# Band selections of a tile in two goes over eight heads each, instead of four goes over four

## What is computed

```python
scores = jnp.einsum('bqhd,bkhd->bhqk', q, k) / jnp.sqrt(d)   # 8 heads, 256 queries, 256 keys
band = jnp.abs(idx[:, None] - idx[None, :]) <= local_size    # 64
scores = jnp.where(band[None, None], scores, neg)
attn = jax.nn.softmax(scores, axis=-1)
o = jnp.einsum('bhqk,bkhd->bqhd', attn, v).reshape(n, t, e)
```

## Time and profile before

| | us |
|---|---|
| median of 3 runs | 968.19 |
| lowest and highest | 966.16, 969.89 |
| span of the profiled execution, first to last instruction | 963.8 |

### The profile page before, as it was taken

How to read it: one execution, slowest core, us unless ns; L and a number is a source line. 1 busy time by engine, 2 the same in 40 slices (tenths; PEclk the granted TensorE clock), 3 DMA queues, 4 the chain that set the end, 5 groups by cost and what they waited for, 6 DMA issues and landing times.

```text
span 963.8 us, 25212 instructions
## 1 busy us (share of the span) xinstructions
PE 871.5 (90%) x9945; PEld 506.2 (53%) x9945; DVE 852.0 (88%) x1719; ACT 740.0 (77%) x1299; POOL 817.8 (85%) x1133
## 2 busy tenths in 40 slices
PE   6588989999999999999999999999999998888874
PEld 3244455555555555555555555555555555544432
DVE  3998888899999999999999999999999998888553
ACT  2546477788888888888888888888888887777751
POOL 4777689999999999999999999999999997656741
PEclk9889899999999999999999999999999999999997
DMA  8000000112211222212112222222212112112233
GB/s 269 1 18 13 7 24 24 29 31 46 47 41 40 51 52 52 51 41 51 39 38 50 51 48 44 51 51 52 51 41 52 39 32 44 41 40 49 46 67 76
DMA packets 109668, 45.59 MB, mean 47 GB/s; under 512 B 89840, under 2 KB 108528, under 8 KB 109552
## 3 DMA queue, kind: packets, MB, share of 16 engines
q1 hardware_dynamic: 109552, 44.00, 20.0%
HBM read 14.09 MB, written 4.19 MB: 19 GB/s over the span
## 4 chain that ended last, share of the span: by engine, by line
DVE 44%; PE 40%; issue 6%; ACT 3%; DMA 2%; SPq 2%; POOL 2%; POOLq 0%; DVEq 0%; ACTq 0%
DVE rowmax L2596 8%; PE ps L592 6%; PE ps L757 6%; PE ps L481 5%; DVE hsplit L2669 4%; DVE prob_a L2534 4%; DVE hid L2656 4%; DVE amax L2525 4%; PE ps L556 3%; PE ps L667 3%; PE ps L723 3%; PE ps L538 3%; PE ps L619 2%; DVE rot L2505 2%; PE ps L677 2%
## 5 line engine op out<-in xcount | busy, mean ns | idle before, releaser
L2596 DVE TENSOR_REDUCE rowmax<-ps 128x4 f32<-128x768 f32 x256 | 243.2, 950 | 23.3 <-PE ps L619 22.6
L1515 ACT ACTIVATE prob<-ps 128x768 f32<-128x768 f32 x256 | 206.9, 808 | 44.5 <-PE ps L647 44.1
L2076 POOL TENSOR_TENSOR hsum<-hsum,minus_half 128x32 f32<-128x32 f32 x32 | 175.7, 5491 | 7.9 <-DVE hsum L2516 7.9
L2113 POOL TENSOR_SCALAR_AFFINE_SELECT prob<-prob 128x256 f32<-128x256 f32 (+1 forms) x256 | 138.5, 541 | 32.2 <-ACT prob L1515 32.2
L2115 POOL TENSOR_SCALAR_AFFINE_SELECT prob<-prob 128x512 f32<-128x512 f32 (+1 forms) x256 | 147.5, 576 | 0.0
L667 PE MATMUL ps<-prob,v_pad 128*32 128x192 f32 x2048 | 103.8, 331 | 1.6 <-POOL prob L2115 1.6
L1490 ACT ACTIVATE high<-ps,bx_col 128x512 f16<-128x512 f32 x128 | 95.2, 769 | 9.1 <-PE ps L592 3.8
L619 PE MATMUL ps<-k_rows,q_rows 24*128 24x192 f16 x1024 | 87.4, 249 | 8.6 <-DVE rowmax L2596 6.7
L647 PE MATMUL ps<-q_rows,k_rows 25*128 25x192 f16 x1024 | 86.8, 247 | 3.2 <-ACT prob L1515 2.5
L592 PE MATMUL ps<-x,wx_qk 64*128 64x256 f32 x512 | 73.4, 404 | 11.5 <-DVE prob_a L2534 11.4
L742 PE MATMUL ps<-wgu,xsplitT 128*128 128x512 bf16 x256 | 66.4, 382 | 12.2 <-ACT v_pad L1501 9.2
(11 more groups left out here) (153 smaller groups left out, 2233.2 us busy)
## 6 DMA issues: line engine op xcount, KB each, us to landing
v_swap<-v_own SPq DMA_DIRECT2D x64, 68.0 KB, 2.0
xin<-in_x SPq DMA_DIRECT2D x32, 128.0 KB, 2.1
enc<-in_ctx SPq DMA_DIRECT2D x32, 128.0 KB, 2.2
out<-yout SPq DMA_DIRECT2D x32, 128.0 KB, 2.0
prob<-in_w_guT SPq DMA_DIRECT2D x4, 512.0 KB, 7.6
prob<-in_w_projT SPq DMA_DIRECT2D x2, 512.0 KB, 9.8
hT<-hsplit SPq DMA_TRANSPOSE x64, 3.1
q_rows<-in_Wkv SPq DMA_DIRECT2D x1, 512.0 KB, 4.0
```

The source lines that it names most:

```text
L1515: copy(prob[:, 2 * c:2 * c + 2, :, :].rearrange("p u a b -> p u (a b)"), ps[:, STB:STB + 2, 0:2 * QW], ACT.Exp, scale=float(XD) ** -0.5).t ...
L2076: g.tensor_tensor(hsum[:, 1, :], hsum[:, 0, :], minus_half[:, :], ALU.pow).then_inc(S["head_pow3"], 1)
L2113: g.affine_select(out=lead, in_=lead, compare_op=ALU.is_ge, fill=0.0, base=BAND - 64 * kb, pattern=[[0, 4], [1, cut]], channel_multiplier=-1)
L2596: v.tensor_reduce(of_head[:, hq:hq + 2, 2 * ng:2 * ng + 2], ps[:, MXB:MXB + 2, 0:2 * QW].rearrange("p j (a b) -> p j a b", a=2), AX, ALU.m ...
```

## The change

`do_sel` covers eight units per call, and a tile has two calls. Each call still issues four affine_selects, now with 512, 1024, 1024 and 512 elements per partition. The first call waits for exp call 4 and the second for exp call 8. In POOL's lists the old calls 0 and 2 are taken out, and the new calls stand where the old calls 1 and 3 stood. `do_val` waits by itself for selection c // 2 + 1 of its tile, so calls 0 and 1 wait for the first and calls 2 and 3 for the second. The order of PE's, DVE's, ACT's and SP's lists is the same.

```diff
             def do_val(t, c):
...
+                pe.wait_ge(S["sel"], t.at(2, c // 2 + 1))
                 g = c % 2
...
             def put_val(t, c):
-                pe.wait_ge(S["sel"], t.at(4, c + 1))
                 do_val(t, c)
...
             def do_sel(t, c):
-                u = slice(4 * c, 4 * c + 4)
+                u = slice(8 * c, 8 * c + 8)
                 for kb, cut in ((0, 64), (1, 128)):
                     lead, trail = prob[:, u, kb, 0:cut], prob[:, u, kb, cut:QW]
                     g.affine_select(out=lead, in_=lead, compare_op=ALU.is_ge, fill=0.0,
-                                    base=BAND - 64 * kb, pattern=[[0, 4], [1, cut]], channel_multiplier=-1)
+                                    base=BAND - 64 * kb, pattern=[[0, 8], [1, cut]], channel_multiplier=-1)
...
             def put_sel(t, c):
-                pool.wait_ge(S["exp"], t.at(8, 2 * c + 2))
+                pool.wait_ge(S["exp"], t.at(8, 4 * c + 4))
                 do_sel(t, c)
...
-                t = at(-7)
-                if t:
-                    put_sel(t, 0)
                 t = at(-5)
                 if t:
                     put_y1_pow(t)
...
                 t = at(-7)
                 if t:
-                    put_sel(t, 1)
+                    put_sel(t, 0)
...
-                t = at(-7)
-                if t:
-                    put_sel(t, 2)
...
                 t = at(-7)
                 if t:
-                    put_sel(t, 3)
+                    put_sel(t, 1)
```

POOL's prologue for tiles 0 to 2, from the change. The lines with a minus are the old calls:

```diff
-            pool.wait_ge(S["exp"], tile[0].at(8, 2))
+            pool.wait_ge(S["exp"], tile[0].at(8, 4))
             do_sel(tile[0], 0)
-            pool.wait_ge(S["exp"], tile[0].at(8, 4))
-            do_sel(tile[0], 1)
...
-            do_sel(tile[0], 2)
             do_y1_pow(tile[3])
             pool.wait_ge(S["exp"], tile[0].at(8, 8))
-            do_sel(tile[0], 3)
+            do_sel(tile[0], 1)
...
-            pool.wait_ge(S["exp"], tile[1].at(8, 6))
-            do_sel(tile[1], 2)
             pool.wait_ge(S["variance"], tile[6].at(1, 1))
             do_head_pow3(tile[6])
             pool.wait_ge(S["y2_stats"], tile[0].at(1, 1))
...
             do_qkn(tile[6])
             pool.wait_ge(S["exp"], tile[1].at(8, 8))
-            do_sel(tile[1], 3)
-            pool.wait_ge(S["exp"], tile[2].at(8, 2))
-            do_sel(tile[2], 0)
+            do_sel(tile[1], 1)
             pool.wait_ge(S["qk"], tile[7].at(1, 1))
             pool.wait_ge(S["qkn"], tile[6].at(1, 1))
             do_rotated(tile[7])
             pool.wait_ge(S["exp"], tile[2].at(8, 4))
-            do_sel(tile[2], 1)
+            do_sel(tile[2], 0)
```

More of the change, by code:

```diff
@@ L1087, in _ @@
             do_o_ps(tile[3])
-            pe.wait_ge(S["sel"], tile[0].at(4, 1))
             do_val(tile[0], 0)
@@ L1109, in _ @@
             do_proj_ps(tile[2], 2)
-            pe.wait_ge(S["sel"], tile[0].at(4, 2))
             do_val(tile[0], 1)
@@ L1129, in _ @@
             do_tr_ps(tile[0], 0)
-            pe.wait_ge(S["sel"], tile[0].at(4, 3))
             do_val(tile[0], 2)
@@ L1157, in _ @@
             do_mx(tile[2], 4)
-            pe.wait_ge(S["sel"], tile[0].at(4, 4))
             do_val(tile[0], 3)
@@ L1167, in _ @@
             do_tr_ps(tile[0], 1)
-            pe.wait_ge(S["sel"], tile[1].at(4, 1))
             do_val(tile[1], 0)
@@ L1191, in _ @@
             do_maxT_ps(tile[2])
-            pe.wait_ge(S["sel"], tile[1].at(4, 2))
             do_val(tile[1], 1)
@@ L1200, in _ @@
             pe.wait_ge(S["ot0"], tile[1].at(1, 1))
-            pe.wait_ge(S["sel"], tile[1].at(4, 3))
             do_val(tile[1], 2)
@@ L1221, in _ @@
             do_pt_ps(tile[5], 0)
-            pe.wait_ge(S["sel"], tile[1].at(4, 4))
             do_val(tile[1], 3)
@@ L1244, in _ @@
             do_aT_ps(tile[5])
-            pe.wait_ge(S["sel"], tile[2].at(4, 1))
             do_val(tile[2], 0)
@@ L1261, in _ @@
             do_mx(tile[3], 6)
-            pe.wait_ge(S["sel"], tile[2].at(4, 2))
             do_val(tile[2], 1)
@@ L1284, in _ @@
             do_val(tile[2], 2)
-            pe.wait_ge(S["sel"], tile[2].at(4, 4))
             do_val(tile[2], 3)
@@ L1328, in _ @@
             do_st(tile[31], 4)
-            pe.wait_ge(S["sel"], tile[31].at(4, 1))
             do_val(tile[31], 0)
@@ L1335, in _ @@
             do_st(tile[31], 5)
-            pe.wait_ge(S["sel"], tile[31].at(4, 2))
             do_val(tile[31], 1)
@@ L1351, in _ @@
             do_down_ps(tile[27])
-            pe.wait_ge(S["sel"], tile[31].at(4, 3))
             do_val(tile[31], 2)
-            pe.wait_ge(S["sel"], tile[31].at(4, 4))
             do_val(tile[31], 3)
@@ L2290, in _ @@
             do_x_pow(tile[7])
-            do_sel(tile[0], 2)
             do_y1_pow(tile[3])
             pool.wait_ge(S["exp"], tile[0].at(8, 8))
-            do_sel(tile[0], 3)
+            do_sel(tile[0], 1)
             pool.wait_ge(S["qkn"], tile[5].at(1, 1))
             do_rotated(tile[6])
-            pool.wait_ge(S["exp"], tile[1].at(8, 2))
+            pool.wait_ge(S["exp"], tile[1].at(8, 4))
             do_sel(tile[1], 0)
-            pool.wait_ge(S["exp"], tile[1].at(8, 4))
-            do_sel(tile[1], 1)
             pool.wait_ge(S["y1"], tile[4].at(1, 1))
@@ L2322, in _ @@
             pool.wait_ge(S["exp"], tile[2].at(8, 4))
-            do_sel(tile[2], 1)
+            do_sel(tile[2], 0)
             do_x_pow(tile[8])
             do_x2_lo(tile[0])
-            pool.wait_ge(S["exp"], tile[2].at(8, 6))
-            do_sel(tile[2], 2)
             pool.wait_ge(S["zr"], tile[1].at(1, 1))
@@ L2332, in _ @@
             pool.wait_ge(S["exp"], tile[2].at(8, 8))
-            do_sel(tile[2], 3)
+            do_sel(tile[2], 1)
             pool.wait_ge(S["y2_stats"], tile[1].at(1, 1))
@@ L2347, in _ @@
             do_x2_lo(tile[29])
+            pool.wait_ge(S["exp"], tile[31].at(8, 4))
             do_sel(tile[31], 0)
-            pool.wait_ge(S["exp"], tile[31].at(8, 4))
-            do_sel(tile[31], 1)
             pool.wait_ge(S["zr"], tile[30].at(1, 1))
@@ L2353, in _ @@
             do_gated(tile[30])
-            pool.wait_ge(S["exp"], tile[31].at(8, 6))
-            do_sel(tile[31], 2)
             pool.wait_ge(S["sqsum"], tile[28].at(1, 1))
@@ L2358, in _ @@
             pool.wait_ge(S["exp"], tile[31].at(8, 8))
-            do_sel(tile[31], 3)
+            do_sel(tile[31], 1)
             pool.wait_ge(S["y2_stats"], tile[30].at(1, 1))
```

2 lines of the change are left out of this document (1 added, 1 removed).

## The result

| | before | after |
|---|---|---|
| median, us | 968.57 | 1023.79 |
| lowest and highest | 966.16, 969.89 | 1021.01, 1024.5 |
| span of the profiled execution | 963.8 | 1019.1 |
| POOL busy | 817.8 | 772.6 |
| step in the middle of the loop | 26.28 | 26.95 |

The changed kernel is slower: 1.0569 times the time of before, with a 95% interval of 1.0543 to 1.0595. POOL does 45 us less work and the kernel takes 55 us more. First the page of after: the busy tenths of POOL, the granted clock in tenths and the chain by engine.

What follows compares the result with a forecast made beforehand. The prediction took the chain through DVE and PE as the bound, with POOL close behind. Span 963.8 + 17 (prologue) + 18 (loop) + 4 (epilogue) = 1003, the median 4.4 above: 1007 us, range 985 to 1026.

Steps and rivals of the forecast that it cites:

- A go: POOL's selects: 1024 elements take 1.07 us and a merged go 3.2 us, with bounds of 2.4 to 3.6.
- PE's waits: Prologue: PE idle for POOL 4 to 5 us at about 123, near 3 at 142, 7 to 8 at about 168.
- The prologue's shift: Prologue: later first selections delay PE's val calls, adding 17 us, 14 to 20 by the bounds of a go.
- the four worked out: Prologue: waits at val 0 and 2 of tile 0, val 2 of tile 1, val 0 of tile 2; shift 16.1.
- at most 2: Prologue: a wait at val 0 of tile 1 and POOL late with the next qkn, not worked out, together at most 2.
- The loop: Each step 0.65 us longer (0.42 to 1.05) by DVE waiting on POOL instructions; 18 us over 28 steps (12 to 29).
- the first term: Loop: rotated ends at 528.8, so L2669 on DVE gets through 0.46 us later, less 0.04 from L2505.
- The epilogue: Tile 31: val 0 comes 3.0 us late and the second go delays val 2 and 3; 4 us, between 2 and 7.
- 1: Rival: the loop hides the longer goes and only prologue and epilogue pay, 989 us; chance 0.23.
- 2: Rival: POOL's queue holds DVE, so less POOL work makes the kernel faster, 959 us at best; chance 0.03.
- 3: Rival: in each step x1_nb is also caught by the 1024-element select, 1.0 us on the chain, 1035 us; chance 0.11.
- 4: Rival: PE's stalls are absorbed everywhere, so no change, 968 us; chance 0.03.

Runs made afterwards that it cites:

- experiment 9: The changed kernel with matmuls of no use ahead of eight val calls, so that PE stays busy in its waits: 1017.38 us, ratio 1.0487.
- experiment 2: Against the kernel before, two goes over eight heads only for tiles 0, 1, 2 and 31, the loop left as before: 1004.33 us, ratio 1.0375.
- experiment 5: The changed kernel with the two 512-element selects ahead of the two of 1024 in each tile's second go: 1024.27 us, ratio 1.0563.
- experiment 4: The changed kernel with each go made of eight selects over four heads at the new places, each half reported when done: 992.25 us, ratio 1.0251.
- experiment 6: The kernel of experiment 5 plus one unread POOL product of 0.73 us ahead of rotated, from tile 9 on: 1010.7 us, ratio 1.0421.
- experiment 7: Against before, only the first go merged (tiles 3 to 30), plus two unread single-column POOL additions ahead of rotated from tile 9: 967.6 us, ratio 0.9996.
- experiment 1: Against the kernel before, two goes over eight heads only for tiles 3 to 30, the other tiles keeping four over four: 992.27 us, ratio 1.0236.

## Why the prediction was right in its range, and where its steps failed

- **Direction and mechanism.** Slower, by waits of PE for selections in the prologue and by DVE behind POOL's instructions in the loop. Both are there. 1023.8 lies 17 above the forecast and 2 below the upper end of the range. That it lies inside is in part luck: the prologue cost 30 us where its bounds were 14 to 20, and the end 10 where they were 2 to 7, and the range held only because the loop, 15 us, stayed far below the 29 that the upper end allowed it.
- **A go.** Forecast 1.07 us for 1024 elements and 3.2 for a go; measured 1.09 and 3.33 (532.74 to 536.07). Right.
- **PE's waits.** Forecast 4 to 5, near 3, and 7 to 8; measured 4.67, 3.50 and 7.91. Right, the second a little short.
- **The prologue's shift was mis-sized: 17 forecast, 30 measured** (25.3 at val 2.0, where 16.1 stood). The waits were summed as if nothing came with them. The five waits sum to 20.3, 3.3 more than the four worked out (4.1, 2.7, 7.9 and 2.3): 1.34 at val 1.0, left as "at most 2", and 0.6 to 0.8 more at val 0.0, 0.2 and 2.0. The other 5 up to val 2.0 lie in a stretch with a clock of 0.74 to 0.83, and with PE kept busy (experiment 9) val 2.0 comes 3.8 earlier; the prediction had no term for the clock. The last 5 come between val 2.0 and h_lo1 of tile 0. The merged goes of the loop are not needed for them: experiment 2, which has none, goes from 24.8 to 31.1 late there. The trace of after shows parts: 2.0 between val 2.0 and the next val call, at a clock of 0.81 from 180 to 200, a wait of 0.90 for `qkn` at 213.06 (named in the prediction, in the same "at most 2"), and 1.27 at val 3.2 (239.77). How the 5 divide was not tried.
- **The loop: 0.65 forecast, 0.67 measured, with the wrong terms.** The match is luck. H_lo1 grew by 0.24, not 0.42. Xn_nb grew by 0.40 (forecast 0 or 0.34). The variance product shrank by 0.25 (forecast 0 or 0.3 more): it got ready 0.45 us before the end of `gated`, and now 0.20 before the end of the go's last select (522.53 and 522.73), and both times it ends 0.04 behind POOL's instruction. X2_nb, which meets a select of 1024 instead of 512, grew by 0.36 and was not in the sum, though its row stood in the earlier trace rows. The rule behind the first term, "rotated ends later, so h_lo1 does", holds for after (experiment 5), but it isn't general: experiments 4, 6 and 7 make rotated end later and the step 0.65 to 0.96 shorter than in the kernels they start from. The steps in the middle give 15 us, not 18, as the late ones, with little work at the front, cost nothing more.
- **The epilogue: 4 forecast, 10 measured.** The first wait is 3.00 as forecast, and the second go of tile 31 adds 1.60. But the second go of tile 30 meets the same end of the pipeline (2.88) and was overlooked, and PE works at a clock of 0.83 from 950 to 990, where the same stretch of before (905 to 945) has 0.91.
- **Rivals.** 1 fell: the loop doesn't hide the goes (experiment 1). 2 fell: POOL's queue was not what held DVE; POOL has 2.4 us of idle time per step and DVE is slower. 3's mechanism, x1_nb blocked as well, isn't there (0.15 us). 4 fell.
- **The Trainium skill's rule** on the pair of ports ("SBUF — State Buffer", section "SBUF: two separate sides": whichever instruction starts first has it for its whole length) was cited as speaking against the change. By that rule the traces agree, and on both sides: h_lo1 ends 1.08 after POOL's product in three kernels, and POOL's product takes 2.13 instead of 1.27 where h_lo1 came first. They don't agree for every pair: beside the long power of head_pow3 a DVE product isn't held up (last section), and there the measurement decides. L2516, which the prediction counts among the products with both inputs in SBUF, has a single column as its second; it ends right behind POOL's instruction like the others. Its strictest reading, the third rival, asked how long POOL's instructions are; the runs show that where their boundaries lie matters as much.

## What to carry to other kernels

When work on one engine is packed into fewer, longer instructions, ask first who waits for the first part of it, above all where the pipeline fills and drains, and look for the lower clock behind each new wait of PE (four of the five in the prologue had it). When two engines block each other by whole instructions, list every pair that runs side by side and find the boundaries between the instructions: here a few tenths of a microsecond decide which engine waits, and a shift can be worth more than the work that is saved. Here the gain on POOL, which wasn't the bound, turned into idle time before its next inputs (2.4 us per step).

## What was not expected of the hardware

- An instruction that is 0.06 us late behind a POOL instruction waits for all of it: 2.29 us against 1.31 with 0.35 us of work put ahead of that instruction, and a step that is 0.96 us longer.
- The blocking goes both ways: POOL's product of 1.27 us takes 2.13 when h_lo1 has come first, and an addition on one column (x_pow, L2036) 1.20 instead of 0.22.
- Not everything on POOL blocks: in after yout_nb (L2660), a product of single columns with two inputs in SBUF, took 0.15 us at 526.06, in the middle of the long power of head_pow3 (524.07 to 529.52).
